# Layer-norm statistics one unit ahead and in pairs, and a fetch of the next batch moved into the MLP, in a windowed-attention block

## The reference

```python
xs = jnp.roll(x, shift=(-SHIFT, -SHIFT), axis=(1, 2))
win = ...                                    # (windows, 64 tokens, 96)
h = _ln(win, ln1_g, ln1_b)
q = jnp.einsum('ntc,chd->nthd', h, wq) + bq  # k and v alike; 3 heads of 32
scores = jnp.einsum('nqhd,nkhd->nhqk', q, k) * (1.0 / np.sqrt(KD))
attn = jax.nn.softmax(scores, axis=-1)
o = jnp.einsum('nhqk,nkhd->nqhd', attn, v)
win = win + jnp.einsum('nqhd,hdc->nqc', o, wo) + bo
h2 = _ln(win, ln2_g, ln2_b)
win = win + jax.nn.gelu(h2 @ w1 + b1, approximate=False) @ w2 + b2
```

## Time and profile before

| | |
|---|---|
| median of 3 runs | 5507.92 us (5507.32 to 5512.99) |
| profiled execution | 5503.1 us, span of the profile 5498.5 us |
| TensorE busy | 4914.6 us, 89% of the span |
| VectorE, ScalarE, GpSimd busy | 4067.4 us (74%), 3932.1 us (72%), 3782.6 us (69%) |
| mean granted TensorE clock | 0.965 of full speed |
| DMA queues | 622.21 MB, 113 GB/s on average |

### The profile page before, as it was taken

One profiled execution on the slowest core, in us unless ns is written; L12 is line 12 of the kernel. 1 busy time (PEld: TensorE's weight loads), 2 busy tenths in 40 slices (PEclk: granted clock), 3 DMA queues, 4 the chain that ended last, 5 costly groups with the idle time before them and its releaser, 6 DMA issues.

```text
span 5498.5 us, 289773 instructions
## 1 busy us (share of the span) xinstructions
PE 4914.6 (89%) x109308; PEld 3995.0 (73%) x109308; DVE 4067.4 (74%) x9010; ACT 3932.1 (72%) x8309; POOL 3782.6 (69%) x4329
## 2 busy tenths in 40 slices
PE   6989989898898988989899898998989989898898
PEld 4677777777776777767777777777777777777776
DVE  7868768687686876868768687776867768677685
ACT  6867668686676866768677686776867768676686
POOL 6867757586575865758667586675866758677576
PEclk9999999999999999999999999999999999999999
DMA  4443333333333333333333334233343333433334
GB/s 123 115 140 95 118 110 107 128 99 123 102 112 126 92 130 101 107 128 98 130 94 114 122 97 138 88 119 116 94 142 95 117 110 101 141 90 124 101 106 135
DMA packets 374339, 622.21 MB, mean 113 GB/s; under 512 B 38745, under 2 KB 240826, under 8 KB 373882
## 3 DMA queue, kind: packets, MB, share of 16 engines
q1 hardware_dynamic: 372320, 617.89, 35.7%
q10 hardware_dynamic: 1562, 0.50, 0.0%
HBM read 309.96 MB, written 308.28 MB: 112 GB/s over the span
## 4 chain that ended last, share of the span: by engine, by line
PE 25%; POOL 21%; issue 19%; DVE 14%; ACT 11%; DMA 5%; ACTq 2%; SPq 2%; DVEq 2%; POOLq 1%
POOL rstd L424 8%; PE psum L610 6%; POOL probs L385 4%; DVE normed L1062 4%; PE psum L734 4%; PE psum L720 3%; DMA h_raw_odd<-turned_rows 3%; PE psum L627 3%; ACT normed L780 3%; PE psum L686 2%; PE psum L658 2%; PE psum L673 2%; DVE stream L1048 2%; DVE stats L965 2%; DVE normed L1069 2%
## 5 line engine op out<-in xcount | busy, mean ns | idle before, releaser
L780 ACT ACTIVATE normed<-stream,shift,rstd 128x96 f32 (+1 forms) x2176 | 828.1, 459 | 662.4 <-POOL shift L433 467.6
L1048 DVE TENSOR_TENSOR stream<-stream,psum 128x384 f32 (+1 forms) x1024 | 562.7, 550 | 511.2 <-PE psum L734 272.3
L392 POOL TENSOR_TENSOR hT_lower<-h_raw_odd,hT_upper 96x512 fp32r<-96x512 f32 x258 | 329.3, 1276 | 679.5 <-ACT hT_upper L792 675.6
L385 POOL TENSOR_TENSOR probs<-probs,prob_inv 128x512 f32<-128x512 f32 x771 | 781.9, 1040 | 0.0
L424 POOL TENSOR_TENSOR rstd<-variance,minus_half 128x16 f32<-128x16 f32 (+2 forms) x249 | 762.8, 3064 | 20.3
L965 DVE BATCH_NORM_STATS2 stats<-stream 128x6 f32 (+2 forms) x4224 | 716.0, 243 | 41.8 <-DVE stream L1048 36.4
L810 ACT ACTIVATE gelu_odd<-psum 128x512 f32<-128x512 f32 x768 | 422.5, 597 | 440.5 <-PE psum L658 435.2
L1019 DVE TENSOR_REDUCE row_max<-psum 128x8 f32<-128x512 f32 x771 | 521.4, 676 | 114.4 <-PE psum L643 114.4
L734 PEld LDWEIGHTS psum<-w_w,gelu_odd 128*64 128x64 f32 x12288 | 528.8, 141 | 80.1 <-issue 80.1
L720 PE MATMUL psum<-h2T_even_upper,w_split_upper 128*128 128x512 f32 x768 | 352.0, 458 | 252.6 <-DVE h2T_even_lower L1086 251.1
L734 PE MATMUL psum<-w_w,gelu_odd 128*64 128x96 f32 x12288 | 552.6, 251 | 19.7 <-ACT gelu_odd L865 19.7
(11 more groups left out here) (99 smaller groups left out, 11290.3 us busy)
## 6 DMA issues: line engine op xcount, KB each, us to landing
turned_rows<-probs SPq DMA_DIRECT2D x416, 384.0 KB, 2.4
h_raw_odd<-turned_rows SPq DMA_DIRECT2D x241, 384.0 KB, 3.9
stream<-in_x SPq DMA_DIRECT2D x272, 192.0 KB, 3.6
h_raw_even<-turned_rows SPq DMA_DIRECT2D x130, 384.0 KB
out<-stream SPq DMA_DIRECT2D x256, 192.0 KB
stream<-in_x SPq DMA_DIRECT2D x272, 180.0 KB
out<-stream SPq DMA_DIRECT2D x256, 180.0 KB
oT<-turned_rows SPq DMA_DIRECT2D x112, 384.0 KB
```

The lines of the kernel that those rows point to most:

```text
L385: nc.gpsimd.tensor_tensor(block_h, block_h, inv, ALU.mult).then_inc(probs_ready, 1)
L392: nc.gpsimd.tensor_tensor(lower[:, tokens], h_raw[parity][0:C, tokens], upper[:, tokens], ALU.subtract).then_inc(hT_copied, 1)
L780: last = nc.scalar.activation(normed1[:, t, :], stream[:, slot, t * C:(t + 1) * C], ACT.Identity, bias=shift1[:, index, t:t + 1], scale=rs ...
L1048: nc.vector.tensor_tensor(part, part, psum[:, banks[g], 0:GROUP], ALU.add).then_inc(added, 1)
```

## The change

It has four parts, in the words of the code:

1. Statistics of the first norm are taken one unit earlier: VectorE takes unit 3 of the next batch in attention step 5, and in MLP step j unit j + 4 instead of j + 3. GpSimd's `finish1` in attention step 7 covers two units (2 and 3) instead of one.
2. In the MLP GpSimd's finishes stand at the head of a step, ahead of the b2 add and the lower copy: `finish2` in pairs in steps 1, 3, 5 and 7, and `finish1` in pairs in steps 2, 4, ..., 12. There are 16 finishes per batch instead of 15.
3. ScalarE copies the upper part of unit j + 2 (the rounding to fp32r) ahead of the whole norm, not between its halves.
4. SyncE fetches unit 3 of the next batch in MLP step 13 instead of at the head of the next attention. The wait for the stores moves behind that place, to step 0 of the next attention (ahead of its load), and after the last batch to the end.

The first batch's attention is changed to match. The core of the diff:

```diff
-LN_CALLS = 15
+LN_CALLS = 16
...
                     if i < BATCH - 1:
                         send_h1(batch + BATCH + i + 1, turned1_late)
+                    if i == BATCH - 3:
+                        for ready in h2T_ready:
+                            wait_apart(sp, ready, batch + BATCH - 1)
+                        fetch_h1(batch + BATCH + AHEAD, 1)
                     store(batch_row + i // 2, i % 2)
-
-                wait_apart(sp, stored, 16 * sum(LOAD_DMAS) * (batch_row + BATCH_ROWS))
...
-                    fetch_h1(batch + s + 3, (s + 3) % 2)
+                    if s > 0:
+                        fetch_h1(batch + s + 3, (s + 3) % 2)
+                    else:
+                        wait_apart(sp, stored, 16 * sum(LOAD_DMAS) * batch_row)
                     row = batch_row + BATCH_ROWS + s // 2
                     load(row, row & (WROWS - 1), s % 2)
...
                     if s == 7:
-                        finish1(call + 2, batch + BATCH + 2, 2, 1)
+                        finish1(call + 2, batch + BATCH + 2, 2, 2)
...
                 for j in range(BATCH):
+                    if j in (1, 3, 5, 7):
+                        finish2(call, batch + j + 7, j + 7, 2)
+                        call = call + 1
+                    if j in (2, 4, 6, 8, 10, 12):
+                        finish1(call, batch + BATCH + j + 2, j + 2, 2)
+                        call = call + 1
                     if j < BATCH - 1:
                         add_b2(batch + j + 1)
                     if j < BATCH - 2:
                         copy_h2T_lower(b, j + 2, batch + j + 2, j % 2)
-                    if j in (1, 3, 5, 7, 9, 11):
-                        at = AHEAD + j - 1
-                        finish1(call, batch + BATCH + at, at, 2)
-                        call = call + 1
-                    if j == 12:
-                        finish1(call, batch + 2 * BATCH - 1, BATCH - 1, 1)
-                    if j in (2, 6):
-                        at = 8 + (j - 2)
-                        finish2(call, batch + at, at, LN_GROUP)
-                        call = call + 1
...
                     gelus(batch + j + 1, 1 - odd, 0)
-                    if norm:
-                        normalise1(batch + BATCH + j + 1, j + 1, range(TILES // 2))
                     copy_h2T_upper(batch + j + 2, odd)
                     if norm:
-                        normalise1(batch + BATCH + j + 1, j + 1, range(TILES // 2, TILES))
+                        normalise1(batch + BATCH + j + 1, j + 1)
...
-                        if 2 <= s < 2 + AHEAD:
+                        if 2 <= s < 3 + AHEAD:
                             n = s - 2
                             statistics1(batch + BATCH + n, n, b * BATCH_ROWS + BATCH_ROWS + n // 2, n % 2)
...
-                    statistics1(batch + BATCH + AHEAD + j, AHEAD + j, batch_row + BATCH_ROWS + row, half)
+                    if row is not None:
+                        statistics1(batch + BATCH + AHEAD + 1 + j, AHEAD + 1 + j, batch_row + BATCH_ROWS + row, half)
```

More of the change, by code:

```diff
@@ L371, in _ @@
                 mlp_traffic(batch_row)
+            wait_apart(sp, stored, 16 * sum(LOAD_DMAS) * BATCHES * BATCH_ROWS)
         @block.gpsimd
@@ L484, in _ @@
             FIRST_CALLS = 15
-            BATCH_0_CALLS = FIRST_CALLS + 9
+            BATCH_0_CALLS = FIRST_CALLS + 10
             def first_attention():
@@ L499, in first_attention @@
                         finish1(next(calls), BATCH, 0, 2)
-                    if s == 11:
-                        finish1(next(calls), BATCH + 2, 2, 1)
+                    if s == 12:
+                        finish1(next(calls), BATCH + 2, 2, 2)
                     if s == 3:
@@ L770, in absent, with normalise1 @@
                 return isinstance(u, int) and u < 0
-            def normalise1(u, index, tiles=range(TILES)):
-                if tiles[0] == 0:
-                    wait_apart(act, rstd1_ready, u + 1)
-                    if not (isinstance(u, int) and u == 0):
-                        wait_apart(act, h1_turned, u)
+            def normalise1(u, index):
+                wait_apart(act, rstd1_ready, u + 1)
+                if not (isinstance(u, int) and u == 0):
+                    wait_apart(act, h1_turned, u)
                 slot = u % SLOTS if isinstance(u, int) else u & (SLOTS - 1)
-                for t in tiles:
+                for t in range(TILES):
                     last = nc.scalar.activation(normed1[:, t, :], stream[:, slot, t * C:(t + 1) * C], ACT.Identity,
                                                 bias=shift1[:, index, t:t + 1], scale=rstd1[:, index, t:t + 1])
-                if tiles[-1] == TILES - 1:
-                    last.then_inc(ln1_ready, 1)
+                last.then_inc(ln1_ready, 1)
             def copy_hT_upper(u, parity, g):
@@ L1118, in first_attention @@
                             constant_rows(*halves)
-                    if s + 8 < BATCH + AHEAD:
+                    if s + 8 < BATCH + AHEAD + 1:
                         first_statistics(s + 8)
@@ L1179, in mlp @@
                 for j in (0, 1, 2):
-                    mlp_step(j, j % 2, (j + 3) // 2, 1 - j % 2, False)
-                mlp_step(3, 1, 3, 0, True)
+                    mlp_step(j, j % 2, 2 + j // 2, j % 2, False)
+                mlp_step(3, 1, 3, 1, True)
                 with dve.Fori(2, 6) as k:
                     for odd in (0, 1):
-                        mlp_step(2 * k + odd, odd, k + 1 + odd, 1 - odd, True)
-                mlp_step(12, 0, 7, 1, True)
+                        mlp_step(2 * k + odd, odd, k + 2, odd, True)
+                mlp_step(12, 0, None, None, True)
                 for j in (BATCH - 3, BATCH - 2, BATCH - 1):
```

## The result

The changed kernel takes 5036.69 us as a median (5033.9 to 5038.26, 4 runs), against 5508.31 us for the kernel before in the same session (5507.32 to 5512.99, 4 runs): a ratio of 0.9142, with a 95% interval of 0.9126 to 0.9158. The prediction was 5030 us (4955 to 5200). Its profiled execution took 5033.9 us with a span of 5029.7, 468.8 us less than the span before.

What follows compares the result with a forecast made beforehand. It took TensorE to set the pace, losing time to waits in the MLP and at attention's start. 386 + 127 - 35 = 478 us off the profiled 5503.1 gave 5025, or 5030 us as a median (4955 to 5200).

Steps and rivals of the forecast that it cites:

- The MLP, 24.1 us per batch: Ten MLP steps: 26.6 us lost to idling and low clock, all regained but 0.25 per step; 386 us over 16 batches.
- The residual, 0.25 us per step: Ten MLP steps: one in six pays 1.4 us for VectorE colliding with GpSimd; bounds 0 and 1.4.
- the first rival: MLP: VectorE, hit by GpSimd, becomes the bound; ten steps last 9.8 us each, 5214 us; chance 0.17.
- GpSimd's step: MLP steps 1 to 8: mean near 9.1 us, so GpSimd falls behind by 5.6 us against 9 us of slack.
- The start of attention, 8.5 us: First two attention steps: the earlier fetch of unit 3 gains 8.5 us per start, 15 times, 127 us; bounds 0 and 9.8.
- The 0.8 us per start: Start of attention: some 0.8 us of ScalarE's stall stays, waiting for the fetch of unit 4.
- The second rival, the moved stall: Start of attention: the fetch of unit 4 comes as late as unit 3's did, 127 us not gained, 5157 us; chance 0.10.
- The additions to attention, 2.2 us: Attention steps 5 and 7: extra statistics cost 1.3 us, the finish of two units 0.85; 35 us with the first attention.
- First attention: The first attention of the run: 2 us added.
- VectorE as the bound: MLP: ten steps of 9.8 us each, shown by a subtraction mean over 2.5 us; +184, 5214 us; chance 0.17.
- GpSimd as the bound: MLP: short finish instructions take 1.0 us each, steps 14.7, 42 us lost per MLP, about 5658 us; chance 0.05.

Runs made afterwards that it cites:

- e4: The changed kernel with the second norm's finishes in two calls of four, at MLP steps 1 and 5: 5031.44 us, ratio 0.9132.
- e10: The changed kernel with SyncE's send before the second three stores, unit 3's statistics in attention step 6, and the second norm's finishes in fours: 5023.72 us.
- e6: The changed kernel with SyncE sending the next batch's normed unit ahead of the second three stores of odd MLP steps: 4998.65 us, ratio 0.9078.
- e8: The changed kernel with SyncE's send ahead of the second three stores and unit 3's statistics in attention step 6: 4985.3 us, ratio 0.9055.
- e1: The kernel before with the moved fetch alone (part 4): 5385.77 us, ratio 0.9780.
- e3: The changed kernel with part 3 undone, the rounding copy back between the halves of the norm: 5191.52 us, ratio 0.9428.
- e5: The kernel before with parts 3 and 4 alone, the finishes keeping their old places: 5142.75 us, ratio 0.9339.
- e7: The changed kernel with unit 3's statistics in attention step 6 instead of step 5: 5021.49 us, ratio 0.9115.
- e9: The changed kernel with one more power in each of the ten finishes of an MLP: 5503.87 us, ratio 0.9990.

## Why the prediction was right, point by point

**The MLP, 24.1 us per batch.** Measured 23.5 (134.14 against 157.64), and the waits that the prediction named are those that went: the shift, the idle time, the low clock. The order of their shares was not told. The text gave the lead the first place and the norm's new place the third; alone, the third part is worth more (243 us against 194), because it cuts the loop of late norm, late copy and late finish. The second part, pairs in place of fours, is worth nothing in the changed kernel (e4) and 38 us once the send is early (e10).

**The residual, 0.25 us per step, for collisions of VectorE and GpSimd.** The size is right, (86.9 - 84.1) / 10 = 0.28, and collisions by themselves are not the cause. This is the step that failed. The subtraction did fall from 1968 to 1373 ns, as the argument against the first rival had it, but the scale behind it rose from 1094 to 1677: the two together took 3.06 us per unit and now take 3.05. The collisions moved and did not grow. Of the 2.8 us left per MLP, e6 removes 2.1 by moving one DMA in SyncE's queue, which the prediction had not looked at inside the MLP. e6 does not part the two cleanly: there the two instructions take 2.84 us per unit (1385 and 1456 ns), 0.21 less for each of the 13 units of a batch, so the collisions shrank along with the wait. But 0.94 us over the undisturbed 1.90 is left per unit, and the steps are at 8.41 all the same. That the size came out right is luck.

The Trainium skill (SBUF — State Buffer, section "Who interferes with whom") states that VectorE and GpSimd exclude each other on their shared port pair; the e10 rows agree with it, the scale from 1879.66 ending 0.82 us after the second add (1882.46), and a copy of 1.28 us that takes 2.01 beside the subtraction. Which of the two goes first they do not settle: that scale started 0.98 us ahead of the add and ended behind it. Beside GpSimd's power the trace differs from the rule:

```profile
1858.63 2.91 POOL L430 TENSOR_TENSOR rstd<-variance,minus_half 128x16 f32<-128x16 f32 x1
...
1860.40 0.95 DVE L1060 TENSOR_TENSOR normed<-stream,mean 128x768 f32 x1
```

In the changed kernel 66 of the 416 subtractions and scales lie wholly inside a power, and none of them takes more than 0.96 us.

**GpSimd's step.** Predicted at a mean near 9.1 us, with a lag of 5.6 against 9 of slack. In the changed kernel the lower copies of MLP steps 0 and 8, eight steps apart, start at

```profile
1805.30 1.28 POOL L480 TENSOR_TENSOR h2T_even_lower<-h_raw_odd,h2T_even_upper 96x512 fp32r<-96x512 f32 x1 [0.74 <-ACT h2T_even_upper L874]
...
1882.04 1.27 POOL L480 TENSOR_TENSOR h2T_even_lower<-h_raw_odd,h2T_even_upper 96x512 fp32r<-96x512 f32 x1
```

which is 9.59 us per step (76.74 / 8) and 9.5 of lag over the eight: all of the slack. GpSimd waits for no other engine between the two. The term was too small by 4 us, and the conclusion held by a hair. In e8 it shows: in the list of waits TensorE waits for that copy in 10 places, 0.9 us at most, and VectorE for the b2 add in 15:

```profile
DVE stream L1046 <- POOL stream L487: 19.2, 15, 1.8
PE psum L722 <- POOL h2T_even_lower L480: 9.1, 10, 0.9
```

Step 9, at 9.26 us on average, is the one MLP step of e8 that is still long.

**The start of attention, 8.5 us.** Measured by e1: 8.63 per attention. The three first steps went from 17.08, 11.84 and 9.87 us (means over 15) to 9.86, 9.87 and 10.39 in the changed kernel; the half microsecond that the third lost was not foreseen, and its cause is open. The 0.8 us per start that were to stay for unit 4 did not come: the waits for h_raw_even sum to 12.4 us over the run, against 11.1 before. The second rival, the moved stall, did not come: that fetch left at 1947.37, 11.1 us after the first scores, while ScalarE's copy of its block started at 1953.69 without a wait.

**The additions to attention, 2.2 us.** After against e1: 174.52 - 172.31 = 2.21. The step of the statistics takes 1.01 more (10.62 to 11.63) and the step behind the finish of two units 0.81 (9.87 to 10.68), with 0.30 between them. e3, which has both, shows the same three steps at 11.63, 10.48 and 10.69, and e5, which has neither, at 10.62, 10.18 and 9.86. e7 takes the first away and leaves the second.

**First attention**, 3.3 us against 2, a single reading. Over all traces it takes 250.8 to 252.4 us without the additions and 252.3 to 254.7 with them. The sum was 478 us, measured 469.

**The rivals.** VectorE as the bound: the longest of the ten steps has a mean of 9.26 us over the batches, not 9.8, and the subtraction is far from 2.5. GpSimd as the bound: not at the cost it has, but e9 shows how near it is, some 3 us per finish away from losing everything.

What stays open: how much of e6's 2.1 us is the shorter wait and how much the fewer collisions, and how far the earlier statistics alone would have carried. The early send was not tried on e3's kernel.

## What to carry to other kernels

A wait that stands in an in-order queue ahead of work that the bounding engine needs is worth moving behind it, even before the wait itself is made shorter: that cut a loop through three engines and was worth more than the earlier data. When a stage runs close to the bounding engine's rate, follow each small remaining wait back to its end, DMA issues included: here two transfers in the wrong order on SyncE were worth 38 us. And an edit that costs nothing while another wait covers it has to be measured again when that wait is gone, as the block of four shows (0 and then 38 us).

## What the runs showed of the hardware

SyncE's issuing takes time that counts: three stores cost 2.00 us (1857.80 in the changed kernel), and an urgent transfer stands behind them. The 9.63 us of the eight at 1931.46 are not all issuing: nothing is issued between the second, which ends at 1933.19, and the third, at 1936.95.

GpSimd's short instructions on 128 x 16 elements mostly take 0.20 to 0.24 us (in e10 from 1886.71 on), and up to 2.02 where VectorE works on two inputs beside them (1887.09 there); its power takes 2.9 us on 16 columns and 5.44 on 32.

The granted clock of TensorE followed the pauses: 0.965 over the run before, 0.998 after, 0.968 in e9, where the pauses are back, with the same matmuls in all of them.

Between the last store before and the first fetch behind it, SyncE stood still from 2107.63 to 2114.27. In the changed kernel, where only the load still waits for the stores, it starts 3.75 us after the last of them is issued (1941.09 to 1944.84). The turn of SyncE's loop lies in both stretches and does not make the difference: from its branch to the next record 2.5 us pass before and 2.6 in the changed kernel (means of 14 turns). Before, 1.2 us more pass ahead of the branch, where the wait for the stores stands, and 2.0 more behind it, at the first wait of the loop's body. What those 2.0 us are is open.
